# A state-space scan layer with experts: the whole causal mask inside the exponents' matrix product, in two tiles of 64 columns

## The chip, the core and the metric

One core of one Trainium2 chip runs the whole layer. Its engines are TensorE (PE, matrix products; the loading of the stationary operand is shown apart as PEld), VectorE (DVE), ScalarE (ACT), GpSimd (POOL) and SyncE (SP), which here only issues DMA transfers. The metric is the device time of one execution in microseconds; lower is better. Times of the runs shown are a median over three executions.

## The reference, cut to what matters

The layer is a state-space scan (32 heads, 64 states, head width 8, chunks of 128 steps), a pairwise gate and a mixture of eight experts. The part that the change touches is the scan inside a chunk. For each head and each chunk, `cum` is the running sum of `-dt`, and

```python
CB = jnp.einsum('bcqhn,bckhn->bchqk', C, B)
cumT = jnp.swapaxes(cum, 2, 3)
diff = cumT[..., :, None] - cumT[..., None, :]
mask = jnp.tril(jnp.ones((chunk, chunk), dtype=bool))
decay = jnp.exp(jnp.where(mask, diff, -jnp.inf))
y_intra = jnp.einsum('bchqk,bckhp->bcqhp', CB * decay, xdt)
states = jnp.einsum('bckhn,bckhp->bchpn', B * state_decay[..., None], xdt)
...
y_inter = jnp.einsum('bcqhn,bchpn->bcqhp', C * jnp.exp(cum)[..., None], prev)
```

The input is 4 sequences of 256 steps, so 8 chunks of 128 steps; the products `CB * decay` are 128x128 for each of 32 heads and 8 chunks. Ahead of it stand a projection of the input onto 4,384 rows (a product of 256 by 256 per pair of heads, in three passes of split operands) and a convolution over four steps.

## The kernel before, in words

**Prologue.** The input is normalised and turned, the first projections, z, the time steps `dt`, their running sums `cum` and the turned tokens are made. GpSimd builds constants in this time: the identity, a small table `tab`, the constant rows of the exponents' operands `cl` and `cr`, zeroed buffers, and `causal`, a 128x128 mask of ones and zeros.

**Pairs of heads.** Sixteen pairs `n` of heads follow (`over_pairs`, L249: the first written out, the next in a loop of two, the last three written out). In a pair, a step `u` from 0 to 3 is one head `j = u % 2` and one half `h = u // 2` of the chunks, that is four 128x128 blocks side by side, a tile of 128x512. For each step:

1. `exponents` (L1298) on TensorE: one product of bf16 operands, `cl[q]` (39 rows by 128) times `cr[q]` (39 rows by 512), into `bank[4 + j]`. Rows 0 to 26 carry the three bf16 parts of the running sums of both sides, rows 32 to 38 are "step rows": they add -1e30 to what lies in a block of 16 queries below the diagonal blocks of 16. So the exponent holds the mask for whole blocks of 16, and not inside the diagonal blocks.
2. `decays` (L668) on ScalarE: `dec = exp(bank)`.
3. `b_dot_c` (L1307) on TensorE, once per half: eight fp32 products of 64 rows by 128x128 into banks 2 and 3, in turn on rows 0 to 63 and 64 to 127 of the array.
4. On VectorE (L971): `g = min(dec, 1) * bank[2 + j]`, 128x512.
5. On GpSimd (L497): `g = g * causal`, in place; it raises `masked`.
6. `weigh` (L1248) on TensorE: waits for `masked`, then four fp32 products of `g` (128 rows by 128) with 16 columns each, into four bands of 32 partitions of bank 7.

Beside these steps TensorE makes the next pair's projection (`passes`: four units of six products of 128x128 by 512 columns), whose taps of the convolution are one ScalarE operation (L561) and three VectorE operations (L887) per unit. TensorE also turns B (`turn_b`), makes the new state (`new_state`), applies it (`from_state`) and turns the next weights (`turn_w`). The order on TensorE is written out by hand in `body` (L1330); between two `weigh(n, q, 0)` lies one period. In it, half 1 is `exponents` 2 and 3 and `b_dot_c(n, q, 1)` right behind them, and half 0 is `exponents` 0 and 1 of the next pair and `b_dot_c(n + 1, q, 0)`. The latter waits for the third convolution unit (`tap_done` 12n + 9).

GpSimd's order in a pair is (L492): mask 0, mask 1, `decay_c` (L490: the decayed C for the state), `prepare` (L460: three small copies for the next pair), mask 2, mask 3. In pairs 14 and 15 it also multiplies z by its gate (L503).

SyncE issues per pair: three DMAs into `cl` and one into `cr` (`load_cum`, L299), four of the result `yi` (L325, after the pair's `y` was copied), two `ecx` (L315), one `w_raw` (L290), one `taps` and two `tap_b` (L295, L297). For the first pair it waits for `const_done` 3 (L358), raised by GpSimd when `causal` is there.

**Constants before.** GpSimd writes `tab` as 32x8 and 7x128 values, and copies it out to `cr[0]` (L454, L455); ScalarE copies it to `cr[1]` (L581, L582), after `const_done` 2 and before it splits the first weights.

**After the pairs.** In the last pair (`last_pair`, L1360) TensorE mixes the scan with the output projection: `residual` (L1283) and `onto_o` (L1290). Then come the second normalisation, the router and eight experts.

Of the kernel before, what the change touches and what calls it, by code (L numbers as in the profile page):

```python
# [23 lines left out]
P = 128  # L24
# [11 lines left out]
KD = DM // P  # L36
# [16 lines left out]
BLOCK = 16  # L53
STEP0, STEPS = 32, P // BLOCK - 1


def decoder_layer(nc, x, ctx_in, W_in, conv_w, conv_b, D, z_bias, W_out, xw, xb, Wr, br, gate_bias,
# [8 lines left out]
    with ExitStack() as stack:  # L66
# [10 lines left out]
        tab = sb("tab", [STEP0 + STEPS, P])  # L77
        carry = sb("carry", [P, 2 * P])
        causal = sb("causal", [P, P])
# [39 lines left out]
        cl = [sb(f"cl{i}", [STEP0 + STEPS, 2, P], BF16) for i in range(2)]  # L119
        with ExitStack() as scan:  # L120
            cr = [scan.enter_context(nc.sbuf_tensor(f"cr{i}", [STEP0 + STEPS, 2, T, P], BF16)) for i in range(2)]
            dec = [scan.enter_context(nc.sbuf_tensor(f"dec{i}", [P, HALF], F32)) for i in range(2)]
            g = [scan.enter_context(nc.sbuf_tensor(f"g{i}", [P, HALF], F32)) for i in range(2)]
        uh = sb("uh", [P, 4, HALF], F32R)
        ul = sb("ul", [P, 4, HALF], F32R)
        xp = [sb(f"xp{i}", [P, T, 2, 2 * HD]) for i in range(2)]
# [20 lines left out]
        ewl = [sb(f"ewl{i}", [P, 3, KD, DM], F32R) for i in range(2)]  # L147
# [12 lines left out]
        gt = sb("gt", [P, T, NR, NR])  # L160
        ge = sb("ge", [P, T, NR, NR])
# [17 lines left out]
        def rows_wide():  # L179

            return tab[0:STEP0, 0:T].unsqueeze(1).unsqueeze(3).to_broadcast([STEP0, 2, T, P])

        def steps_wide():

            return tab[STEP0:STEP0 + STEPS, :].unsqueeze(1).unsqueeze(1).to_broadcast([STEPS, 2, T, P])
# [23 lines left out]
        cr1_done, cr0_done = sem("cr1_done"), sem("cr0_done")  # L209
# [15 lines left out]
        g_done, masked, y_done = sem("g_done"), sem("masked"), sem("y_done")  # L225
# [54 lines left out]
        def _(sp):  # L280
# [18 lines left out]
            def load_cum(m, q):  # L299

                at_least(sp, expo_done, 4 * (m - 2))
                for s in range(3):
                    sp.dma_start(cl[q][T * s:T * s + T, :, :],
                                 cum_dram[s, bass.ds(2 * T * (m - 1), 2 * T), :]
                                 .rearrange("(j t) k -> t j k", j=2)).then_inc(cum_in[q], 16)
# [63 lines left out]
            sp.wait_ge(cr0_done, 2)  # L369

# [41 lines left out]
        def _(pool):  # L412
# [11 lines left out]
            rows, steps_of = tab[0:STEP0, 0:T], tab[STEP0:STEP0 + STEPS, :]  # L424
            link(pool.memset(rows, 0.0))
            link(pool.memset(steps_of, NEG))
# [4 lines left out]
            link(pool.affine_select(out=steps_of, in_=steps_of, compare_op=ALU.is_ge, fill=0.0, base=0,  # L431
                                    pattern=[[1, P]], channel_multiplier=-BLOCK))
            link(pool.affine_select(out=steps_of, in_=steps_of, compare_op=ALU.is_ge, fill=0.0, base=BLOCK - 1,
                                    pattern=[[-1, P]], channel_multiplier=BLOCK))
            pool.memset(earlier[:], 1.0).then_inc(const_done, 1)
            for q in (1, 0):
                link(pool.memset(cl[q][:], 1.0))

                link(pool.affine_select(out=cl[q][STEP0:STEP0 + STEPS, :, :], in_=cl[q][STEP0:STEP0 + STEPS, :, :],
                                        compare_op=ALU.is_ge, fill=0.0, base=-BLOCK,  # L440
                                        pattern=[[0, 2], [1, P]], channel_multiplier=-BLOCK))
# [93 lines left out]
        def _(act):  # L535
# [45 lines left out]
            act.copy(cr[1][0:STEP0, :, :, :], rows_wide()).then_inc(cr1_done, 1)  # L581
            act.copy(cr[1][STEP0:STEP0 + STEPS, :, :, :], steps_wide()).then_inc(cr1_done, 1)  # L582
# [519 lines left out]
        def _(pe):  # L1102
# [426 lines left out]
```

## Time and profile before

| what | value |
|---|---|
| time, median of 3 runs (lowest to highest) | 445.43 us (443.49 to 446.92) |
| the profiled execution | 447.58 us |
| its span in the profile | 445.8 us |
| mean granted TensorE clock over the span | 0.976 of full |

The span runs from the first to the last instruction of the profiled execution; 1.8 us of its time lie around it. Busy times are the union of an engine's instructions. A product's record lasts longer than the distance between two products, since products overlap in the array, so distances between starts tell more than durations. Columns of a timeline row are: start in us, length in us, engine, line, operation, written tile <- read tiles, shapes, count merged into the row, and in brackets the idle time before it and what ended it.

### The profile page before, as it was taken

To read this page: it belongs to the slowest core of one execution; us is meant where nothing else is said; L and a number is where in the kernel's file an instruction comes from. 1 tells how busy PE (TensorE), PEld (TensorE's weight loads), DVE (VectorE), ACT (ScalarE), POOL (GpSimd) and SP (SyncE) were. 2 spreads that over 40 slices of the span, in tenths; PEclk is the share of its full clock that TensorE was granted. 3 is DMA by queue.
4 is the path that set the end of the run, shared out by engine and by line. 5 is a ranking of instruction groups with operands and counts; after the bars stand their busy time and mean duration, and the time that the engine had idled before them with its cause. 6 is when DMAs were issued, how large, how long until landed. Compare 5 with 4: busy or idle time off the path is not lost.

```text
span 445.8 us, 8885 instructions
## 1 busy us (share of the span) xinstructions
PE 414.9 (93%) x2959; PEld 318.6 (71%) x2959; DVE 351.1 (79%) x604; ACT 225.7 (51%) x408; POOL 223.3 (50%) x238
## 2 busy tenths in 40 slices
PE   2898999999999999999999977998999999999995
PEld 1686767676667676667676556766789889899885
DVE  3787689889889889889889937947886696786775
ACT  5665545455545545545577430146543653554541
POOL 3444344654544664544577540022738558648661
PEclk9999799999999999999999978999899999999999
DMA  6302101221111212112210040011110201200002
GB/s 189 77 1 53 51 8 53 57 56 55 34 28 50 56 56 56 39 23 51 54 34 32 16 137 2 1 43 50 51 48 24 73 26 45 71 0 1 0 0 96
DMA packets 33607, 20.00 MB, mean 45 GB/s; under 512 B 15816, under 2 KB 31488, under 8 KB 33584
## 3 DMA queue, kind: packets, MB, share of 16 engines
q1 hardware_dynamic: 33584, 19.71, 15.7%
q8 instruction: 13, 0.21, 0.2%
q14 instruction: 10, 0.08, 0.1%
HBM read 17.33 MB, written 1.31 MB: 42 GB/s over the span
## 4 chain that ended last, share of the span: by engine, by line
PE 43%; issue 23%; POOL 14%; DVE 12%; ACT 3%; DMA 2%; SPq 1%; POOLq 1%; DVEq 0%; ACTq 0%
PE bank L1107 30%; POOL g L497 9%; PE bank L1131 4%; DVE conv L887 4%; POOL ce L490 3%; DMA w_raw<-in_L_attn_W_in_dram 1%; PE bank L1315 1%; DVE stats L814 1%; DMA ew_raw<-in_L_ffn_Wdown_dram 1%; ACT conv L561 1%; POOL xp L462 1%; PE bank L1475 1%; PE bank L1293 1%; DVE xres L1006 1%; SPq L325 1%
## 5 line engine op out<-in xcount | busy, mean ns | idle before, releaser
L887 DVE SCALAR_TENSOR_TENSOR conv<-bank,taps,conv 128x510 f32<-128x510 f32 (+2 forms) x204 | 151.6, 746 | 28.3 <-ACT conv L561 23.5
L497 POOL TENSOR_TENSOR g<-g,causal 128x512 f32<-128x512 f32 x64 | 81.6, 1294 | 108.1 <-DVE g L971 108.1
L1131 PE MATMUL bank<-uth,parts 128*128 128x512 f32 x272 | 98.6, 413 | 1.5 <-DVE utl L870 1.0
L561 ACT ACTIVATE conv<-bank,tap_b,taps 128x512 f32<-128x512 f32 x68 | 52.9, 779 | 77.2 <-PE bank L1131 76.8
L523 POOL TENSOR_TENSOR ul<-conv,uh 128x512 fp32r<-128x512 f32 x32 | 42.8, 1353 | 46.6 <-ACT uh L770 33.7
L528 POOL TENSOR_TENSOR parts<-conv,parts 128x512 fp32r<-128x512 f32 x30 | 44.2, 1502 | 36.0 <-ACT parts L784 35.9
L1131 PEld LDWEIGHTS bank<-uth,parts 128*128 128x128 f32 x272 | 51.8, 190 | 10.7 <-issue 1.7
L1131 PE MATMUL bank<-utl,parts 128*128 128x512 f32 x136 | 56.9, 418 | 0.0
L1107 PE MATMUL bank<-ewh,parts 128*128 128x256 f32 x256 | 46.2, 279 | 1.2 <-DVE parts L1094 1.2
L1079 DVE CAST uh<-conv 128x512 fp32r<-128x512 f32 x28 | 26.4, 977 | 22.7 <-ACT conv L766 22.4
L1315 PE MATMUL bank<-conv 64*128 64x128 f32 x512 | 43.4, 289 | 0.3 <-DVE conv L887 0.3
L1315 PEld LDWEIGHTS bank<-conv 64*128 64x128 f32 x512 | 36.7, 191 | 6.8 <-DVE conv L887 5.8
L971 DVE SCALAR_TENSOR_TENSOR g<-dec,bank 128x512 f32<-128x512 f32 x64 | 40.8, 679 | 0.2 <-ACT dec L672 0.2
L1107 PEld LDWEIGHTS bank<-ewh,parts 128*128 128x128 f32 x256 | 39.6, 188 | 1.9 <-issue 1.6
L1089 DVE TENSOR_TENSOR conv<-conv 128x512 f32<-128x512 f32 x32 | 32.4, 1037 | 8.2 <-ACT conv L789 8.1
L1107 PE MATMUL bank<-ewl,parts 128*128 128x256 f32 x128 | 35.7, 279 | 0.0
L672 ACT ACTIVATE dec<-bank 128x512 f32<-128x512 f32 x64 | 34.5, 592 | 0.0
L1258 PE MATMUL bank<-g,xp 128*16 128x128 f32 x512 | 27.3, 284 | 5.7 <-POOL g L497 5.6
L1131 PEld LDWEIGHTS bank<-utl,parts 128*128 128x128 f32 x136 | 26.0, 191 | 8.8 <-issue 6.3
L766 ACT ACTIVATE conv<-bank,eb 128x512 f32<-128x512 f32 x32 | 20.1, 689 | 18.3 <-POOL eb L520 12.0
L691 ACT CAST ewh<-ew_raw 128x512 fp32r<-128x512 f32 x24 | 13.4, 617 | 30.7 <-PE bank L1107 22.4
L1062 DVE SCALAR_TENSOR_TENSOR xres<-bank,prob,xres 128x256 f32<-128x256 f32 x64 | 26.2, 472 | 2.2 <-PE bank L1107 2.2
(204 smaller groups left out, 744.0 us busy)
## 6 DMA issues: line engine op xcount, KB each, us to landing
w_raw<-in_L_attn_W_in_dram SPq DMA_DIRECT2D x17, 256.0 KB, 3.2
ecx<-ecum_dram SPq DMA_DIRECT2D x32, 128.0 KB, 2.9
ew_raw<-in_L_ffn_Wup_dram SPq DMA_DIRECT2D x7, 256.0 KB, 2.8
ew_raw<-in_L_ffn_Wgate_dram SPq DMA_DIRECT2D x7, 256.0 KB, 3.1
ew_raw<-in_L_ffn_Wdown_dram SPq DMA_DIRECT2D x7, 256.0 KB, 3.8
xres<-in_x_dram SPq DMA_DIRECT2D x2, 512.0 KB, 4.1
out_dram<-xres SPq DMA_DIRECT2D x4, 256.0 KB, 2.3
yi<-yev SPq DMA_DIRECT2D x60, 16.0 KB, 1.9
```

Source lines behind the costliest of these rows:

```text
L497: pool.tensor_tensor(g_v, g_v, causal[:].unsqueeze(1).to_broadcast([P, 4, P]), ALU.mult).then_inc(masked, 1)
L523: pool.tensor_tensor(ul[:, v, :], u32[:, v, :], f32(uh[:, v, :]), ALU.subtract).then_inc(ul_done, 1)
L528: pool.tensor_tensor(el[:, v, :], e32[:, v, :], f32(eh[:, v, :]), ALU.subtract).then_inc(el_done, 1)
L561: act.activation(conv[q][:, j, HALF * h:HALF * (h + 1)], bank[u % 2][:], ACT.Identity, bias=tap_b[q][:, j:j + 1], scale=taps[q][:, j, TAPS ...
L672: act.activation(dec[b][:], bank[4 + b][:], ACT.Exp).then_inc(exp_done, 1)
L887: dve.scalar_tensor_tensor(out=dst[:, :, d:SEQ], in0=src[:, :, 0:SEQ - d], scalar=taps[q][:, j, TAPS - 1 - d:TAPS - d], in1=dst[:, :, d:SE ...
L971: dve.scalar_tensor_tensor(out=g[b][:], in0=dec[b][:], scalar=1.0, in1=bank[2 + b][:], op0=ALU.min, op1=ALU.mult).then_inc(g_done, 1)
L1089: dve.tensor_tensor(e32[:, v, :], e32[:, v, :], u32[:, v, :], ALU.mult).then_inc(e_done, 1)
L1107: ins = pe.matmul(dst, left, right, start=(k == 0 and i == 0), stop=(k == n - 1 and i == 2))
L1131: ins = pe.matmul(bank[u % 2][:], w, x_t, start=(i == 0), stop=(i == 3 * KD - 1))
L1258: ins = pe.matmul(y_bank(n, h)[32 * i:32 * i + 2 * HD, P * h:P * (h + 1)], xp[q][:, 4 * h + i, j, :], g[j][:, i * P:(i + 1) * P], start=fi ...
L1315: ins = pe.matmul(bank[2 + j][:, i * P:(i + 1) * P], conv[q][r, 0, s], conv[q][r, 1, s], start=True, stop=True)
```

## The change

The step rows grow from 7 to 64 and `tab`, `cl` and `cr` from 39 to 96 rows. Each exponents' tile is formed by two products: keys 0 to 63 (partitions 0 to 63 of the bank) with `cr[q][0]`, and keys 64 to 127 (partitions 64 to 127) with `cr[q][1]`. Each has 96 rows, 64 stationary columns and 512 moving columns. GpSimd's multiplication by `causal` is removed, with `causal` and `masked`; `weigh` now waits for `g_done` of VectorE. `cr` is now four tiles instead of two, and GpSimd fills three of them. Each `load_cum` has five DMAs instead of four.

```diff
-BLOCK = 16
-STEP0, STEPS = 32, P // BLOCK - 1
+STEPS = NS
+ROWS = STEPS + 32
...
-        tab = sb("tab", [STEP0 + STEPS, P])
+        tab = sb("tab", [ROWS, 2, P])
-        causal = sb("causal", [P, P])
...
-        cl = [sb(f"cl{i}", [STEP0 + STEPS, 2, P], BF16) for i in range(2)]
+        cl = [sb(f"cl{i}", [ROWS, 2, P], BF16) for i in range(2)]
-            cr = [scan.enter_context(nc.sbuf_tensor(f"cr{i}", [STEP0 + STEPS, 2, T, P], BF16)) for i in range(2)]
+            cr = [[scan.enter_context(nc.sbuf_tensor(f"cr{i}_{a}", [ROWS, 2, T, P], BF16)) for a in range(2)]
+                  for i in range(2)]
...
+        ewl1 = sb("ewl1", [P, 3, KD, DM], F32R)
+        gt = sb("gt", [P, T, NR, NR])
+        ge = sb("ge", [P, T, NR, NR])
...
-                sp.dma_start(cr[q][24:27, :, :, :].rearrange("s j t k -> s (j t k)"),
-                             cum_dram[:, bass.ds(2 * T * (m - 1), 2 * T), :]
-                             .rearrange("s r k -> s (r k)")).then_inc(cum_in[q], 16)
+                for a in range(2):
+                    sp.dma_start(cr[q][a][STEPS + 3 * T:STEPS + 3 * T + 3, :, :, :].rearrange("s j t k -> s (j t k)"),
+                                 cum_dram[:, bass.ds(2 * T * (m - 1), 2 * T), :]
+                                 .rearrange("s r k -> s (r k)")).then_inc(cum_in[q], 16)
...
-            sp.wait_ge(cr0_done, 2)
...
-            rows, steps_of = tab[0:STEP0, 0:T], tab[STEP0:STEP0 + STEPS, :]
+            rows, steps_of = tab[STEPS:ROWS, 0, 0:T], tab[0:STEPS, :, :]
+            pool.wait_ge(const_done, 1)
...
-            link(pool.memset(causal[:], 1.0))
-            pool.affine_select(out=causal[:], in_=causal[:], compare_op=ALU.is_ge, fill=0.0,
-                               base=0, pattern=[[1, P]], channel_multiplier=-1).then_inc(const_done, 1)
+            for q, a in ((1, 1), (0, 0), (0, 1)):
+                link(pool.tensor_copy(cr[q][a][STEPS:ROWS, :, :, :], rows_wide()))
+                last_one = pool.tensor_copy(cr[q][a][0:STEPS, :, :, :], steps_wide(a))
+                if (q, a) != (0, 1):
+                    link(last_one)
+            last_one.then_inc(const_done, 1)
             pool.wait_ge(const_done, 3)
-            pool.tensor_copy(cr[0][0:STEP0, :, :, :], rows_wide()).then_inc(cr0_done, 1)
-            pool.tensor_copy(cr[0][STEP0:STEP0 + STEPS, :, :, :], steps_wide()).then_inc(cr0_done, 1)
-            pool.wait_ge(cr0_done, 2)
...
-                    pool.wait_ge(g_done, 4 * (n - 1) + u + 1)
-                    g_v = g[u % 2][:].rearrange("p (i k) -> p i k", k=P)
-                    pool.tensor_tensor(g_v, g_v, causal[:].unsqueeze(1).to_broadcast([P, 4, P]),
-                                       ALU.mult).then_inc(masked, 1)
...
-            act.copy(cr[1][0:STEP0, :, :, :], rows_wide()).then_inc(cr1_done, 1)
-            act.copy(cr[1][STEP0:STEP0 + STEPS, :, :, :], steps_wide()).then_inc(cr1_done, 1)
+            act.copy(cr[1][0][STEPS:ROWS, :, :, :], rows_wide()).then_inc(cr1_done, 1)
+            act.copy(cr[1][0][0:STEPS, :, :, :], steps_wide(0)).then_inc(cr1_done, 1)
...
-                pe.wait_ge(masked, a + 1)
+                pe.wait_ge(g_done, a + 1)
...
-                    pe.wait_ge(cum_in[q], 64 * (k + q))
+                    pe.wait_ge(cum_in[q], 80 * (k + q))
                 at_least(pe, exp_done, 4 * (n - 1) + u - 1)
-                pe.matmul(bank[4 + j][:], cl[q][:, j, :], cr[q][:, j, 4 * h:4 * h + 4, :].rearrange("p t k -> p (t k)"),
-                          start=True, stop=True).then_inc(expo_done, 1)
+                for a in range(2):
+                    ins = pe.matmul(bank[4 + j][NS * a:NS * (a + 1), :], cl[q][:, j, NS * a:NS * (a + 1)],
+                                    cr[q][a][:, j, 4 * h:4 * h + 4, :].rearrange("p t k -> p (t k)"), start=True, stop=True)
+                ins.then_inc(expo_done, 1)
```

The rest of the diff writes the new constants (one selection less on `tab`, one small fill more, the table twice as wide), and lets `ewl1`, `gt` and `ge`, which only the experts use, share the memory of the scan's tiles.

## Rows read from the trace of the kernel before

**Rows 1.** The page: busy time by engine; the mask's group and the exponential's.
```profile
PE 414.9 (93%) x2959; PEld 318.6 (71%) x2959; DVE 351.1 (79%) x604; ACT 225.7 (51%) x408; POOL 223.3 (50%) x238
...
L497 POOL TENSOR_TENSOR g<-g,causal 128x512 f32<-128x512 f32 x64 | 81.6, 1294 | 108.1 <-DVE g L971 108.1
```

**Rows 2.** Waits of the whole span: engine line <- releaser: us, times, longest.
```profile
PE bank L1258 <- POOL g L497: 5.6, 15, 0.4
```

**Rows 3.** Stretches from `weigh(n, q, 0)` to the next: busy us by engine, clock.
```profile
53.28:66.58 13.30, 12.91 (x116) 9.18 (x117) 11.86 (x18) 6.86 (x13) 6.83 (x9) 1.00 0.03 6
...
145.04:158.34 13.30, 12.92 (x118) 9.18 (x117) 11.81 (x18) 6.87 (x13) 6.84 (x8) 1.00 0.18 47
226.20:239.48 13.28, 12.91 (x116) 9.17 (x116) 11.76 (x18) 11.12 (x23) 10.56 (x12) 1.00 0.10 26
```

**Rows 4.** Timeline of TensorE in one pair, 144.5 to 158.5 us.
```profile
145.39 0.61 PE L1131 MATMUL bank<-uth,parts 128*128 128x512 f32 x2
146.38 0.41 PE L1258 MATMUL bank<-g,xp 128*16 128x128 f32 x8 [0.38 <-POOL g L497]
146.73 0.50 PE L1131 MATMUL bank<-utl,parts 128*128 128x512 f32 x1
147.07 0.39 PE L1131 MATMUL bank<-uth,parts 128*128 128x512 f32 x1
147.39 0.39 PE L1304 MATMUL bank<-cr,cl 39*128 39x512 bf16 x1
147.40 0.49 PE L1315 MATMUL bank<-conv 64*128 64x128 f32 x2
147.62 0.38 PE L1304 MATMUL bank<-cr,cl 39*128 39x512 bf16 x1
147.83 1.05 PE L1315 MATMUL bank<-conv 64*128 64x128 f32 x14
148.82 0.41 PE L1258 MATMUL bank<-g,xp 128*16 128x128 f32 x8
...
152.44 0.62 PE L1131 MATMUL bank<-uth,parts 128*128 128x512 f32 x2
152.99 0.41 PE L1258 MATMUL bank<-g,xp 128*16 128x128 f32 x8
...
154.44 0.60 PE L1304 MATMUL bank<-cr,cl 39*128 39x512 bf16 x2
154.91 1.16 PE L1315 MATMUL bank<-conv 64*128 64x128 f32 x16
156.01 0.41 PE L1258 MATMUL bank<-g,xp 128*16 128x128 f32 x8
```

**Rows 5.** Timelines of VectorE, GpSimd and SyncE in the same pair.
```profile
152.55 2.31 DVE L887 SCALAR_TENSOR_TENSOR conv<-bank,taps,conv 128x510 f32<-128x510 f32 x3 [0.74 <-ACT conv L561]
...
157.59 1.27 DVE L971 SCALAR_TENSOR_TENSOR g<-dec,bank 128x512 f32<-128x512 f32 x2
...
158.35 1.28 POOL L497 TENSOR_TENSOR g<-g,causal 128x512 f32<-128x512 f32 x1 [4.52 <-DVE g L971]
...
150.73 0.27 SPq L306 DMA_DIRECT2D cr<-cum_dram  x1
```

**Rows 6.** Timeline of TensorE in the prologue: L1180, four column bands at a time.
```profile
19.44 0.64 PE L1180 MATMUL bank<-uth,wa 128*32 128x256 f32 x8
19.89 0.61 PE L1180 MATMUL bank<-utl,wa 128*32 128x256 f32 x8
```

**Rows 7.** Timeline of TensorE behind the last pair: L1293, one after another.
```profile
266.95 3.62 PE L1293 MATMUL bank<-woT,yi 128*128 128x256 f32 x16
```

**Rows 8.** Timelines of GpSimd, ScalarE and SyncE in the prologue.
```profile
16.00 1.88 POOL L454 CAST cr<-tab 32x2048 bf16<-32x2048 f32 x1
...
9.00 0.59 ACT L553 CAST parts<-bank 128x512 fp32r<-128x512 f32 x1 [1.43 <-PE bank L1117]
...
36.66 0.95 SPq L303 DMA_DIRECT2D cl<-cum_dram  x3
```

**Rows 9.** Timelines of the last pair: TensorE, GpSimd.
```profile
264.17 0.50 PE L1278 MATMUL bank<-ce,state 128*16 128x128 f32 x4
264.78 0.41 PE L1258 MATMUL bank<-g,xp 128*16 128x128 f32 x8
...
262.23 2.50 POOL L497 TENSOR_TENSOR g<-g,causal 128x512 f32<-128x512 f32 x2 [5.38 <-DVE g L971]
```

**Rows 10.** The page, DMA issues: KB each, median us from issue to landing.
```profile
ecx<-ecum_dram SPq DMA_DIRECT2D x32, 128.0 KB, 2.9
```

More of the change, by code:

```diff
@@ L146, in decoder_layer @@
         ewh = [sb(f"ewh{i}", [P, 3, KD, DM], F32R) for i in range(2)]
-        ewl = [sb(f"ewl{i}", [P, 3, KD, DM], F32R) for i in range(2)]
+        ewl = [sb("ewl0", [P, 3, KD, DM], F32R), ewl1]
         eh = parts[:, 0:4, :]
@@ L159, in decoder_layer @@
         bg = sb("bg", [P, T, NR])
-        gt = sb("gt", [P, T, NR, NR])
-        ge = sb("ge", [P, T, NR, NR])
         sel = sb("sel", [P, T, NR])
@@ L179, in rows_wide, with steps_wide @@
         def rows_wide():
-            return tab[0:STEP0, 0:T].unsqueeze(1).unsqueeze(3).to_broadcast([STEP0, 2, T, P])
-        def steps_wide():
-            return tab[STEP0:STEP0 + STEPS, :].unsqueeze(1).unsqueeze(1).to_broadcast([STEPS, 2, T, P])
+            return tab[STEPS:ROWS, 0, 0:T].unsqueeze(1).unsqueeze(3).to_broadcast([ROWS - STEPS, 2, T, P])
+        def steps_wide(a):
+            return tab[0:STEPS, a, :].unsqueeze(1).unsqueeze(1).to_broadcast([STEPS, 2, T, P])
         def zgate(v):
@@ L208, in decoder_layer @@
         const_chain, const_done = sem("const_chain"), sem("const_done")
-        cr1_done, cr0_done = sem("cr1_done"), sem("cr0_done")
+        cr1_done = sem("cr1_done")
         dve_chain, act_chain = sem("dve_chain"), sem("act_chain")
@@ L224, in decoder_layer @@
         expo_done, exp_done, cb_done = sem("expo_done"), sem("exp_done"), sem("cb_done")
-        g_done, masked, y_done = sem("g_done"), sem("masked"), sem("y_done")
+        g_done, y_done = sem("g_done"), sem("y_done")
         b_turned, b_read, st_done, st_read = sem("b_turned"), sem("b_read"), sem("st_done"), sem("st_read")
@@ L302, in load_cum @@
                 for s in range(3):
-                    sp.dma_start(cl[q][T * s:T * s + T, :, :],
+                    sp.dma_start(cl[q][STEPS + T * s:STEPS + T * s + T, :, :],
                                  cum_dram[s, bass.ds(2 * T * (m - 1), 2 * T), :]
                                  .rearrange("(j t) k -> t j k", j=2)).then_inc(cum_in[q], 16)
-                sp.dma_start(cr[q][24:27, :, :, :].rearrange("s j t k -> s (j t k)"),
-                             cum_dram[:, bass.ds(2 * T * (m - 1), 2 * T), :]
-                             .rearrange("s r k -> s (r k)")).then_inc(cum_in[q], 16)
+                for a in range(2):
+                    sp.dma_start(cr[q][a][STEPS + 3 * T:STEPS + 3 * T + 3, :, :, :].rearrange("s j t k -> s (j t k)"),
+                                 cum_dram[:, bass.ds(2 * T * (m - 1), 2 * T), :]
+                                 .rearrange("s r k -> s (r k)")).then_inc(cum_in[q], 16)
             def load_ecx(m, q):
@@ L423, in _ @@
                                base=0, pattern=[[-1, P]], channel_multiplier=1).then_inc(const_done, 1)
-            rows, steps_of = tab[0:STEP0, 0:T], tab[STEP0:STEP0 + STEPS, :]
+            rows, steps_of = tab[STEPS:ROWS, 0, 0:T], tab[0:STEPS, :, :]
+            pool.wait_ge(const_done, 1)
             link(pool.memset(rows, 0.0))
-            link(pool.memset(steps_of, NEG))
+            link(pool.memset(steps_of, 0.0))
             for s in range(3):
@@ L430, in _ @@
                                         pattern=[[-1, T]], channel_multiplier=1))
[L431 to L434, printed above, removed]
+            link(pool.affine_select(out=steps_of, in_=steps_of, compare_op=ALU.not_equal, fill=NEG, base=0,
+                                    pattern=[[-(STEPS - 1), 2], [1, P]], channel_multiplier=-1))
+            link(pool.memset(tab[0:1, 1, 0:STEPS], NEG))
             pool.memset(earlier[:], 1.0).then_inc(const_done, 1)
@@ L437, in _ @@
                 link(pool.memset(cl[q][:], 1.0))
-                link(pool.affine_select(out=cl[q][STEP0:STEP0 + STEPS, :, :], in_=cl[q][STEP0:STEP0 + STEPS, :, :],
-                                        compare_op=ALU.is_ge, fill=0.0, base=-BLOCK,
-                                        pattern=[[0, 2], [1, P]], channel_multiplier=-BLOCK))
+                lower = cl[q][0:STEPS, :, :].rearrange("r j (a k) -> r j a k", a=2)
+                link(pool.affine_select(out=lower, in_=lower, compare_op=ALU.is_ge, fill=0.0, base=-1,
+                                        pattern=[[0, 2], [1, 2], [1, STEPS]], channel_multiplier=-1))
             pool.wait_ge(xn_done, 4)
```

## The prediction

> **What bounds the kernel now.** I read the page first. GpSimd's multiplication by the mask is its largest group, 64 operations of 1.294 us, 81.6 us in all, yet GpSimd is busy for only half of the span and TensorE for 93% [rows 1]. So the question is not how much is removed but how much of it anyone waits for. The waits answer that: TensorE's products of L1258 (`weigh`) stood idle for the mask 15 times, 5.6 us in all, at most 0.4 us [rows 2]. Next I cut the span into stretches from one `weigh(n, q, 0)` to the next. The first and the last of the fourteen last 13.30 and 13.28 us; TensorE is busy for 12.92 of 13.30 us, VectorE for 11.81, GpSimd for 6.84, and the granted clock is 1.00 [rows 3]. Only TensorE is near its limit, and what is missing is the one idle of 0.38 us in front of the first `weigh` of each pair [rows 4].
>
> The timeline gives that stall more exactly. In the passes two products start 0.22 to 0.23 us apart (the row at 145.39 is 0.61 long with two records of 0.39), and a `weigh` that waits for nothing starts 0.32 us after the last pass (152.44 + 0.23 = 152.67, `weigh` at 152.99). Ahead of the stalled one the last pass starts at 145.61, so it could start at 145.93 and does at 146.38: 0.45 us [rows 4]. The chain behind it is VectorE's `g` 0 and 1 at 157.59, the mask from 158.35 to 159.63, and the next `weigh` 13.30 after 146.38, at 159.68 [rows 4, 5]. The other three `weigh` of a pair wait for no mask. TensorE's own work in a period is therefore 13.30 - 0.45 = 12.85 us.
>
> **What is removed.** The stall, 0.45 us per period. `g` 0 is ready by 157.59 + 0.7 = 158.3 (two take 1.27), and TensorE reaches `weigh` at 159.23 (12.85 after 146.38), so VectorE's result is 0.9 us early and no new wait takes the place of the old one [rows 5]. VectorE itself is idle for 1.49 us of the period [rows 3], 0.74 of it in front of the third convolution unit [rows 5], so it could follow a period down to 13.30 - 0.74 = 12.56.
>
> **What is added on TensorE.** 64 products become 128, each of 64 stationary columns and 512 moving columns in bf16. Whether the two of a tile run side by side decides the sign. The nearest row is L1180, where four fp32 products with 32 columns each, in four bands of output partitions, read four different moving operands: a group of eight records starts 0.45 us after the previous one [rows 6]. The same 256 moving columns in fp32 on the whole array cost 3.62 / 8 = 0.45 us per product (16 records are eight products) [rows 7]. So four side by side took the time of one. `weigh` says the same at 128 columns. I take it that two bands of 64 columns run side by side too: an exponents' tile then costs 0.23 us as before (147.39 to 147.62) [rows 4]. The other end is one after the other, 0.46 us.
>
> What isn't free is the change of the array's shape. Before, the exponents (39 rows) and `b_dot_c` (64 rows) both use row halves and all columns. The trace shows two `b_dot_c` records starting at 147.40, beside the first exponents' product at 147.39, and only 14 left at 147.83: half 1 takes 148.82 - 147.39 = 1.43 us. In half 0, where `b_dot_c` starts behind the exponents, it alone takes 156.01 - 154.91 = 1.10 us, and the half takes 1.57 [rows 4]. With 96 rows the exponents fill all row groups, so that overlap ends: 1.57 instead of 1.43, +0.14. Then there is one more change of shape per half, between exponents and `b_dot_c`. A change costs 0.09 to 0.13 by the rows: `weigh` follows a pass by 0.32 instead of 0.23, and the pass behind it starts 0.35 after it (146.38 to 146.73) where its products alone are about 0.22, half of what L1180 takes for twice the columns [rows 4, 6]. I take 0.11 to 0.12 for each. Half 1: +0.14 + 0.11 = +0.25. Half 0: +0.12. Together +0.37 us per period. Bounds: +0.14 if changes of shape cost nothing, and about +0.8 if each also exposes the loading of weights at both ends of the exponents (0.1 a time, four times).
>
> The Trainium skill, "TensorEngine Tiling (Array Packing)", section "Tiling Modes", says that changing the tiling mode, not just the tile, drains the engine. The trace agrees with 0.09 to 0.13 us at each change of form; without the rule the sum would be 0.23 us a period better.
>
> New period: 12.85 + 0.37 = 13.22 us against 13.30, so -0.08, fourteen times: -1.1 us. Does another limit come first? The third convolution unit starts its VectorE part 0.25 us later relative to `weigh` 0 and ends at 154.86 + 0.25 = 155.11, while TensorE reaches `b_dot_c` 0 at 154.91 + 0.37 = 155.28 [rows 4, 5], so TensorE stays the limit by 0.17.
>
> **What is added on the other queues.** SyncE's `load_cum` gets one DMA more, 0.27 us of issue. The last of them ends at 150.73 + 0.27 = 151.00, now 151.27, and TensorE needs the data at 154.44 [rows 4, 5]: 3.2 us are left for it to land, so I cost it at nothing. If that cover were gone, each pair would wait for the difference. In the prologue ScalarE fills `cr[1][0]` before it splits the first weights, and stood idle for 1.43 us in front of that [rows 8]. GpSimd's start grows by a few tenths (a table twice as wide, a wait, a fill more; a selection less), within these 1.43. GpSimd then fills three tiles with six copies of 1.88 us instead of one with two [rows 8]: from about 16 us to 27.5, and the mark that SyncE needs for the first `load_cum` is read at 36.66 [rows 8]. Cost zero, with 9 us of cover. The first pair pays its added products at the start (two halves, +0.4, since its first half runs at a slower spacing) and loses its own stall (-0.3): +0.1.
>
> **The end of the pairs.** The stretch from `weigh(15, q, 0)` to the last pair's `b_dot_c` has half 1 in it: +0.25. In the last pair the masks 2 and 3 end at 262.23 + 2.50 = 264.73 and the last `weigh` starts at 264.78, behind two products that start at 264.17 [rows 9] and need about 0.27. Without the mask it starts at 264.44: -0.34, and TensorE's output projection behind it carries that on.
>
> **Sum** against the profiled execution: -1.1 + 0.1 + 0.25 - 0.34 = -1.1 us, 447.58 to 446.5. That execution lay 2.15 us above the median of the runs shown, so on the median: 445.43 - 1.1 = 444.3 us. About 1% (4.5 us) is what a measurement of this kernel can tell from no change; this is no change.
>
> **Rivals.**
> (a) The two column tiles run one after the other. The place is L1304's successor, the price 0.23 us per exponents' tile, 0.92 per period: 13.22 + 0.92 = 14.14, fourteen times +0.84 = +11.8, with the first and the fifteenth pair some +13.5, so 459 us. It decides from about 0.1 us per tile that isn't hidden: sixty-four tiles then cost 6 us, more than 1% of the time. Against it stands L1180 [rows 6, 7]; for it, that no row has bf16 with two bands of 64.
> (b) They run side by side, but each pair of them costs about 0.1 more, by an exposed load of weights or a late start of the second: four tiles, +0.4 per period, 13.62: +4.5 + 0.5, so some 449.5 us. The Trainium skill, "TensorE: Matmul & The Clock Gate", Part 3, gives 2.38 times for three column tiles at 512 columns; as an estimate from that page two tiles would cost some 0.05 more than one, +0.2 per period, 447.5 us. L1180 speaks against it.
> (c) Changes of shape are nearly free and `b_dot_c` loses only its overlap: +0.14, period 12.99, -0.31 fourteen times, -4.3, with the ends -5: 440.5 us. The 0.32 between pass and `weigh` speaks against it.
> (d) The fifth DMA makes the sums late: landing would have to take over 3.2 us where `ecx`, ten times its size, lands in 2.9 [rows 10]; a delay of 0.3 per pair gives 448.5.
>
> **Chances.** Forecast 0.55 (its own range 442 to 447.5), (a) 0.12, (b) 0.16, (c) 0.14, (d) 0.03. Faster by over 1% (below 441.0) is two thirds of (c), 0.10. Slower by over 1% (above 449.9) is (a) and half of (b), 0.20. The rest, 0.70, is within 1%. The range from 440.3 to 451 leaves out (a) and the edges.
>
> **What would show it.** Right: a period of 13.1 to 13.3 us; no wait of L1258 for anything; two exponents' records per tile starting within 0.05 us; half 1 about 1.7 us and half 0 about 1.7 us long; GpSimd's busy time down by some 82 us, up by 8 in the prologue. Wrong: exponents' records 0.2 us apart (rival a), a first `weigh` that now waits for VectorE, or a period below 13.0. Then the step at fault would be the cost of a change of shape, which I read from three distances only.

## The result, and the profile after

The changed kernel takes 443.81 us (median of 20 runs, 440.28 to 445.62) where the kernel before, run beside it, takes 445.86 us (median of 20, 443.49 to 449.06). The ratio is 0.9945 with a 95% interval of 0.9925 to 0.9966: 0.55% faster, 2.5 us, between 1.5 and 3.3. The prediction was 444.3 us on a median of 445.43, so -1.1 us forecast and -2.5 measured. By the bound of 1% it is no change, as forecast; with 20 runs on each side it can be told from none.

The page first: busy time by engine, and the groups that answer to [rows 1].

```profile
PE 415.7 (94%) x3023; PEld 314.9 (71%) x3023; DVE 348.5 (79%) x604; ACT 225.6 (51%) x408; POOL 150.6 (34%) x176
...
L491 POOL TENSOR_TENSOR ce<-conv,ecx 128x512 f32<-128x512 f32 x16 | 20.9, 1306 | 157.7 <-DVE conv L884 157.7
L1255 PE MATMUL bank<-g,xp 128*16 128x128 f32 x512 | 27.7, 284 | 0.0
```

GpSimd fell from 223.3 to 150.6 us (81.6 of mask gone, 8.9 come in, 7.5 of it four more copies of constants). That is worth next to nothing by itself. TensorE has 64 products more and nearly the same busy time (414.9 us before, 415.7 now). The last row is the effect: `weigh` (now L1255) has no idle time before it, where it stood 5.6 us in fifteen waits [rows 2].

The chain that ended last, by engine, has no GpSimd in it any more, where GpSimd had 14% of it before:

```profile
PE 84%; DVE 9%; DMA 3%; ACT 2%; issue 1%; SPq 1%; DVEq 0%; ACTq 0%
```

The stretches from one `weigh(n, q, 0)` to the next, as in [rows 3]: length, busy us of PE, PEld, DVE, ACT and POOL, clock, DMA.

```profile
52.94:66.11 13.17, 13.17 (x121) 9.05 (x120) 11.75 (x17) 6.83 (x14) 1.46 (x3) 1.00 0.04 8
131.98:145.15 13.17, 13.17 (x121) 9.05 (x120) 11.76 (x17) 6.86 (x14) 1.75 (x5) 1.00 0.18 48
224.20:237.37 13.17, 13.17 (x122) 9.05 (x121) 11.76 (x17) 11.11 (x22) 8.34 (x11) 1.00 0.12 29
```

A period lasts 13.17 us instead of 13.30, and TensorE is busy in all of it. The starts of the first and the fifteenth `weigh(n, q, 0)`, 52.94 and 237.37, give 13.174 over fourteen periods. So the stall of 0.45 us is gone and 0.32 us of work on TensorE has taken its place. TensorE's timeline in one pair shows where (as [rows 4], 132 to 142 us).

```profile
131.98 0.41 PE L1255 MATMUL bank<-g,xp 128*16 128x128 f32 x8
132.32 0.50 PE L1128 MATMUL bank<-utl,parts 128*128 128x512 f32 x1
132.66 0.40 PE L1128 MATMUL bank<-uth,parts 128*128 128x512 f32 x1
132.98 0.62 PE L1302 MATMUL bank<-cr,cl 96*64 96x512 bf16 x4
133.54 1.16 PE L1314 MATMUL bank<-conv 64*128 64x128 f32 x16
134.63 0.41 PE L1255 MATMUL bank<-g,xp 128*16 128x128 f32 x8
...
140.28 0.62 PE L1302 MATMUL bank<-cr,cl 96*64 96x512 bf16 x4
140.83 1.16 PE L1314 MATMUL bank<-conv 64*128 64x128 f32 x16
141.92 0.41 PE L1255 MATMUL bank<-g,xp 128*16 128x128 f32 x8
```

Four exponents' products and the change of shape behind them take 0.56 us (132.98 to 133.54) where two products took 0.44 in half 1 (147.39 to 147.83) and 0.47 in half 0 [rows 4]: the two bands run side by side. The two records of a tile start within 0.02 us of each other. All sixteen records of `b_dot_c` now stand behind the exponents, none beside them. Half 1 lasts 134.63 - 132.98 = 1.65 us (1.43 before) and half 0 141.92 - 140.28 = 1.64 (1.57 before): +0.22 and +0.07, +0.29 in all.

### The profile page after: what moved, and what is told of

It reads as the page before. It is cut to its first block, busy times and chain, and to the rows that moved or that the text cites. A ratio compares the mean times of both kernels' runs of the same rounds, so it can differ in the third digit from the quotient of the medians.

```text
span 443.9 us, 8932 instructions
## 1 busy us (share of the span) xinstructions
PE 415.7 (94%) x3023; PEld 314.9 (71%) x3023; DVE 348.5 (79%) x604; ACT 225.6 (51%) x408; POOL 150.6 (34%) x176
## 4 chain that ended last, share of the span: by engine, by line
PE 84%; DVE 9%; DMA 3%; ACT 2%; issue 1%; SPq 1%; DVEq 0%; ACTq 0%
PE bank L1104 30%; PE bank L1128 22%; PE bank L1314 8%; PE bank L1255 5%; PE bank L1302 4%; PE bank L1264 3%; PE bank L1322 2%; PE bank L1114 2%; PE bank L1275 2%; DVE conv L884 2%; DMA w_raw<-in_L_attn_W_in_dram 1%; PE bank L1290 1%; DMA ew_raw<-in_L_ffn_Wdown_dram 1%; DVE stats L811 1%; PE bank L1474 1%
## 5 line engine op out<-in xcount | busy, mean ns | idle before, releaser
L491 POOL TENSOR_TENSOR ce<-conv,ecx 128x512 f32<-128x512 f32 x16 | 20.9, 1306 | 157.7 <-DVE conv L884 157.7
L1104 PE MATMUL bank<-ewh,parts 128*128 128x256 f32 x256 | 47.2, 282 | 1.2 <-DVE parts L1091 1.2
L1314 PEld LDWEIGHTS bank<-conv 64*128 64x128 f32 x512 | 31.7, 191 | 13.7 <-issue 7.2
L1314 PE MATMUL bank<-conv 64*128 64x128 f32 x512 | 37.9, 288 | 0.3 <-DVE conv L884 0.3
L688 ACT CAST ewh<-ew_raw 128x512 fp32r<-128x512 f32 x24 | 13.4, 618 | 33.1 <-PE bank L1104 24.4
L1255 PE MATMUL bank<-g,xp 128*16 128x128 f32 x512 | 27.7, 284 | 0.0
```

The source lines that it names most:

```text
L1104: ins = pe.matmul(dst, left, right, start=(k == 0 and i == 0), stop=(k == n - 1 and i == 2))
L1255: ins = pe.matmul(y_bank(n, h)[32 * i:32 * i + 2 * HD, P * h:P * (h + 1)], xp[q][:, 4 * h + i, j, :], g[j][:, i * P:(i + 1) * P], start=fi ...
L1314: ins = pe.matmul(bank[2 + j][:, i * P:(i + 1) * P], conv[q][r, 0, s], conv[q][r, 1, s], start=True, stop=True)
```

## The experiments

Each kernel is measured beside runs of the kernel before on the same chip; where its own number of runs is small (4 to 6 for most), the period in its trace, fourteen times repeated, tells more than its median.

### 1. What the mask alone cost

The kernel before without GpSimd's multiplication; the mask inside the diagonal blocks is left out.

```diff
-                    pool.wait_ge(g_done, 4 * (n - 1) + u + 1)
-                    g_v = g[u % 2][:].rearrange("p (i k) -> p i k", k=P)
-                    pool.tensor_tensor(g_v, g_v, causal[:].unsqueeze(1).to_broadcast([P, 4, P]),
-                                       ALU.mult).then_inc(masked, 1)
...
-                pe.wait_ge(masked, a + 1)
+                pe.wait_ge(g_done, a + 1)
```

> The kernel before, without GpSimd's multiplication (the mask inside the diagonal blocks of 16 is left out of the computation), the exponents as they were. Theory (TensorE's order bounds the pairs, the mask cost one stall of 0.45 us a pair): the period falls from 13.30 to 12.85 us, no wait takes the stall's place, fourteen times -0.45 and the ends some -0.6, so about 439 us, ratio 0.985. Rival (VectorE or a DMA takes over): a new idle before the first weigh or before b_dot_c, period 13.0 to 13.2, 442 to 444 us.

437.06 us, ratio 0.9784 (0.9729 to 0.9838). The stretch of all fourteen periods, with the same columns as above:

```profile
51.92:231.65 179.73, 179.73 (x1625) 128.62 (x1624) 164.62 (x238) 100.01 (x191) 30.32 (x60) 1.00 0.17 44
```

179.73 / 14 = 12.84 us, against 12.85 expected. TensorE is busy throughout and nothing takes the stall's place. This is the most that a free mask could bring in the periods: 0.46 us each, 6.5 us. The change brought 0.13 each. The median fell by more than that, 8.5 us; in this trace the last pair is 3.0 us shorter as well (22.65 us against 25.64), and the part on the last pair, behind the experiments, says why that stretch varies.

### 2. What the new exponents alone cost

The changed kernel with the mask's multiplication, its constant and its semaphore put back.

> The changed kernel with GpSimd's multiplication by the mask put back. Theory (the path from weigh 0 over half 1, the third unit's passes, ScalarE, VectorE and the mask back to weigh 0 is one closed chain of 13.30 us, and the new half 1 is 0.22 longer): period 13.52 us, fourteen times +0.22, about 449 us. Rival (the stall of 0.45 us is slack that swallows the added 0.3 us of TensorE): period stays 13.30, 446 us.

450.01 us (ten runs), ratio 1.0082 (1.0048 to 1.0116).

```profile
51.15:240.97 189.82, 185.16 (x1681) 126.73 (x1681) 164.68 (x239) 100.64 (x191) 99.98 (x116) 1.00 0.16 43
```

The stall in front of `weigh` 0 is back; in this kernel `weigh` is L1263 and the mask L502:

```profile
132.50 0.41 PE L1263 MATMUL bank<-g,xp 128*16 128x128 f32 x8 [0.34 <-POOL g L502]
```

189.82 / 14 = 13.56 us, +0.26 against before (+0.22 expected). The stall did not swallow the added work: TensorE is idle again for 0.33 us a period (185.16 of 189.82). So the stall was no slack. It closed a chain in which half 1 itself stands (`weigh` 0, half 1, the third unit's passes, its convolution, `g` 0, the mask, `weigh` 0), and what is added to half 1 comes out again behind the mask. Half 0 stands beside that chain: VectorE still works on the convolution when its `b_dot_c` is done. Its 0.07 us are missing from the 0.26, which fits. Exponents +0.26 with the mask, +0.33 without (13.17 against 12.84), mask +0.46 with the old exponents and +0.39 with the new.

### 3. Do the two bands run side by side?

Both products of a tile sent to the same partitions, hence to the same columns of the array (the exponents of keys 64 to 127 go astray).

```diff
-                    ins = pe.matmul(bank[4 + j][NS * a:NS * (a + 1), :], cl[q][:, j, NS * a:NS * (a + 1)],
+                    ins = pe.matmul(bank[4 + j][0:NS, :], cl[q][:, j, NS * a:NS * (a + 1)],
```

> The changed kernel with both exponents' products of a tile sent to partitions 0 to 63 of the bank, so that they use the same column band and must run one after the other (the exponents of keys 64 to 127 are left out of the right place). Theory (two bands run side by side and save the whole second product): each of four tiles costs 0.22 us more, period 13.17 + 0.9 = 14.07 us, about 457 us. Rival (the bands only overlap in part): under 0.15 us per tile, period below 13.8, below 453 us.

456.34 us, ratio 1.0214 (1.0154 to 1.0275). TensorE's timeline of one half:

```profile
130.11 1.05 PE L1302 MATMUL bank<-cr,cl 96*64 96x512 bf16 x4
131.09 1.16 PE L1314 MATMUL bank<-conv 64*128 64x128 f32 x16
132.19 0.41 PE L1255 MATMUL bank<-g,xp 128*16 128x128 f32 x8
```

The four products take 0.98 us until `b_dot_c` starts, against 0.56 side by side: 0.42 more for two tiles, 0.21 a tile, which is a whole product. The period is (247.52 - 51.34) / 14 = 14.01 us, 14.07 expected. So the bands save a whole product; rival (a) is refuted, and it would have cost 0.84 us a period (14.01 against 13.17) where the prediction said 0.92. Experiment 4 has the other comparison, two bands against one product.

### 4. Rows or bands: what costs the 0.3 us?

One product of 96 rows and 128 columns in place of the two (the mask of keys 64 to 127 is wrong).

```diff
-                for a in range(2):
-                    ins = pe.matmul(bank[4 + j][NS * a:NS * (a + 1), :], cl[q][:, j, NS * a:NS * (a + 1)],
-                                    cr[q][a][:, j, 4 * h:4 * h + 4, :].rearrange("p t k -> p (t k)"), start=True, stop=True)
+                ins = pe.matmul(bank[4 + j][:], cl[q][:, j, :],
+                                cr[q][0][:, j, 4 * h:4 * h + 4, :].rearrange("p t k -> p (t k)"), start=True, stop=True)
```

> The changed kernel with one product per tile, 96 rows and all 128 columns, on the first of the two cr tiles (the mask of keys 64 to 127 is left out). The array keeps the shape of the passes, so the change of shape between passes and exponents falls away and the one before b_dot_c stays. Theory (what the change costs TensorE is the lost overlap with b_dot_c plus one more change of shape of about 0.1 us per half): period 13.17 - 0.2 = 12.97 us, about 441 us. Rival (the loss is all in the overlap, shape changes between passes and exponents are free): period 13.1 to 13.2, 443 to 444 us.

439.05 us, ratio 0.9848 (0.9789 to 0.9907).

```profile
128.99 0.41 PE L1255 MATMUL bank<-g,xp 128*16 128x128 f32 x8
129.91 0.61 PE L1301 MATMUL bank<-cr,cl 96*128 96x512 bf16 x2
130.44 1.16 PE L1313 MATMUL bank<-conv 64*128 64x128 f32 x16
131.54 0.41 PE L1255 MATMUL bank<-g,xp 128*16 128x128 f32 x8
...
137.08 0.61 PE L1301 MATMUL bank<-cr,cl 96*128 96x512 bf16 x2
137.64 1.16 PE L1313 MATMUL bank<-conv 64*128 64x128 f32 x16
138.73 0.41 PE L1255 MATMUL bank<-g,xp 128*16 128x128 f32 x8
```

From `weigh` to the exponents it is 0.92 us instead of 1.00: the change of shape between passes and exponents is gone, 0.08. But from the exponents to the next `weigh` it is 1.63 in half 1 and 1.65 in half 0, nearly the changed kernel's 1.65 and 1.64 and not the 1.43 and 1.57 of before. Counted from the exponents on, the 96 rows alone lengthen the halves: the sixteen records of `b_dot_c` stand behind the exponents here too. The halves leave out what lies in front of the exponents, though, and there the bands cost something. The period is (232.87 - 51.10) / 14 = 12.98 us, 12.97 expected, so the three kernels without a mask form a ladder:

| exponents | period us | step |
|---|---|---|
| 39 rows, 128 columns (experiment 1) | 12.84 | |
| 96 rows, 128 columns (this one) | 12.98 | +0.14, the rows |
| 96 rows, two bands of 64 columns (the change) | 13.17 | +0.19, the bands |

The rows cost 0.14 us, the overlap of `b_dot_c` with the exponents. They add no change of shape: the one in front of the exponents moves behind them. The bands bring the second change of shape in each half, and that is the larger part of the 0.33.

### 5. The same stall, removed by order alone

If the mask costs one stall in front of `weigh` 0, two passes in between cover it, with the mask where it was. The same move saves a change of shape, and can be made for `weigh` 2 and `from_state` as well. Both moves were put into both kernels.

```diff
-                passes(m, r, 1, range(4))
+                passes(m, r, 1, range(6))
                 weigh(n, q, 0)
-                passes(m, r, 1, range(4, 6))
...
-                passes(m, r, 3, range(4))
+                passes(m, r, 3, range(6))
                 weigh(n, q, 2)
                 from_state(n, 0)
                 from_state(n, 1)
-                passes(m, r, 3, range(4, 6))
```

> The kernel before, mask and all, with the first weigh of a pair moved two passes later, in front of exponents 2 and 3. Theory (the mask cost one stall of 0.45 us, and each change of shape of the array about 0.1): the stall is covered by the two passes (0.46 us) and the array goes from weigh to exponents without the passes between, which saves 0.2 more: period 12.84 - 0.2 = 12.65 us, fourteen times -0.65, about 436.5 us, better than both kernels. Rival (the closed chain over VectorE and GpSimd, 13.30 us, does not get shorter by it): period 13.1 to 13.3, 443 to 446 us.

> The same with weigh 2 and from_state also moved two passes later, in front of the next pair's exponents. Theory: TensorE's own order falls by another 0.2 us to 12.45, but the chain over VectorE and the mask (13.30 - 0.67 = 12.63 us) then sets the period: 12.6 us, about 436 us, and a stall for the mask of 0.1 to 0.2 us is back. Rival (only TensorE's order counts): 12.45 us, 433.5 us.

> The changed kernel with the first weigh moved two passes later. Theory (one change of shape less): period 13.17 - 0.2 = 12.97 us, about 441 us. Rival (changes of shape cost only together with waits, so nothing is gained where weigh doesn't wait): period 13.17, 443.8 us.

> The changed kernel with weigh 0, weigh 2 and from_state two passes later. Theory: two changes of shape less, period 13.17 - 0.4 = 12.77 us, about 438.3 us, still behind the kernel before in the new order. Rival (VectorE's chain, at least 12.6, interferes): 12.9 or more, 440 us.

| kernel | median us (runs) | ratio, interval | period us, expected |
|---|---|---|---|
| before, weigh 0 later | 440.41 (4) | 0.9834, 0.9741 to 0.9927 | 12.78, 12.65 |
| before, both later | 436.70 (4) | 0.9767, 0.9701 to 0.9832 | 12.66, 12.6 |
| after, weigh 0 later | 440.95 (4) | 0.9864, 0.9798 to 0.9930 | 12.93, 12.97 |
| after, both later | 439.01 (4) | 0.9835, 0.9764 to 0.9906 | 12.86, 12.77 |

The stretch of fourteen periods of the kernel before with both moves, and behind it that of the changed kernel with both:

```profile
52.69:229.92 177.23, 176.23 (x1625) 130.77 (x1625) 164.48 (x239) 101.96 (x192) 99.39 (x116) 1.00 0.18 45
```

The changed kernel:

```profile
51.04:231.01 179.97, 179.04 (x1681) 128.89 (x1680) 164.41 (x239) 101.99 (x192) 30.71 (x61) 1.00 0.18 45
```

With the two moves the old kernel, GpSimd's mask and all, has a period of 12.66 us: below the changed kernel's 13.17, and below 12.84, what the mask's removal alone gave. This is not the cover alone, since the moves also save changes of shape: the changed kernel, which had no stall, gains 0.31 by them (13.17 to 12.86).

The first move was 0.13 us a period short of its forecast in the kernel before. The two passes cover the mask but for a rest:

```profile
127.80 0.39 PE L1131 MATMUL bank<-uth,parts 128*128 128x512 f32 x1
128.25 0.41 PE L1258 MATMUL bank<-g,xp 128*16 128x128 f32 x8
```

`weigh` 0 follows the last pass by 0.45 us, where it is 0.32 in the changed kernel in the same order (128.50 to 128.82), and starts 0.07 us after its mask ends (126.89 + 1.29 = 128.18). `weigh` 2 is 0.11 us late in the same way. Half of these 0.24 us come back in half 0, where `b_dot_c` starts 0.36 us after the exponents instead of 0.47. The list of waits shows none of this in the fourteen periods, because the records of the passes last longer than the gap.

On the changed kernel the first move is worth 0.24 us (13.17 to 12.93): that is what going in and out of the passes' shape costs once less. It is more than the 0.1 of one change, because the first pass behind `weigh` also holds up the next one, by 0.34 us instead of 0.23 (132.32 to 132.66 in the timeline of the changed kernel). The second move is worth only 0.07, since now `b_dot_c` 0 waits for the third convolution unit, which VectorE ends at 133.87 + 2.31 = 136.18:

```profile
135.54 0.62 PE L1302 MATMUL bank<-cr,cl 96*64 96x512 bf16 x4
136.23 1.16 PE L1314 MATMUL bank<-conv 64*128 64x128 f32 x16
```

That is 0.69 us instead of 0.55. In the kernel before with both moves it is 0.68 instead of 0.47, and the first `weigh` follows its pass by 0.34. So its period of 12.66 hit the forecast of 12.6, but the wait in it is for VectorE in front of `b_dot_c` and not the one for the mask that was expected.

### 6. The last pair, and the versions that beat both

In the last pair ScalarE stands for the first expert's weights, whose three DMAs wait on SyncE behind the result of pair 15. ScalarE's timeline in the kernel before (L691), the wait in brackets:

```profile
259.90 0.62 ACT L691 CAST ewh<-ew_raw 128x512 fp32r<-128x512 f32 x1 [8.35 <-DMA ew_raw<-in_L_ffn_Wdown_dram]
```

And in the changed kernel (L688):

```profile
258.37 0.62 ACT L688 CAST ewh<-ew_raw 128x512 fp32r<-128x512 f32 x1 [8.75 <-DMA ew_raw<-in_L_ffn_Wdown_dram]
```

The exponentials and everything behind them wait with it. I moved these loads to the end of SyncE's turn for pair 15, in four settings (the definition of `load_expert` moves ahead of the loop with them).

```diff
                 if n + 2 <= PAIRS:
                     load_taps(n + 2, q)
+                if n == PAIRS - 1:
+                    load_expert(0, 0)
...
-            load_expert(0, 0)
```

> The kernel before in the new order of both moves, with the three loads of the first expert's weights issued at the end of pair 15's turn on SyncE instead of behind the last result's DMAs. Theory (in the last pair ScalarE stands 7 to 9 us for these weights, and the exponentials behind it, g, the masks and the last weigh with it): that wait goes, VectorE's gating is next, the last pair gets 3 to 5 us shorter, 432 to 433.5 us. Rival (the stretch is bound by the result's DMAs and VectorE anyway): under 1 us, 436 us.

> The changed kernel in the same order and with the same early loads. Theory: period 12.86 us as without the early loads, so 2.8 us slower than the other in the fourteen pairs, and up to 1.5 us faster in the last pair, where no mask stands between g and the last weigh once the weights are there: 433.5 to 435.5 us. Rival (the last pair hides the masks behind VectorE's gating): the whole 2.8 us stay, 435 to 436.5 us.

> The kernel before in its own order, with only the first expert's weights loaded early. Theory (the wait of ScalarE for these weights ends the last pair, with two masks behind it): period 13.30 us as ever, last pair from weigh(15, q, 0) to the residual some 21.8 us instead of 25.6, about 442.5 us. Rival (something else ends the last pair): over 24 us, 445 us or more.

> The changed kernel in its own order, with only the early loads. Theory (the wait for the weights hid what the masks cost the last pair): period 13.17 us, last pair some 19.0 to 19.3 us, so 1.8 us from the periods and 2.5 us from the last pair ahead of the other kernel of this call, 438 to 439 us. Rival (the change is worth no more than its 2 us in any setting): 440.5 us or more.

| kernel, with the early loads | median us (runs) | ratio, interval | last pair us |
|---|---|---|---|
| before, own order | 443.23 (12) | 0.9948, 0.9927 to 0.9969 | 21.77 |
| after, own order | 439.25 (6) | 0.9858, 0.9828 to 0.9888 | 19.70 |
| before, both later | 435.64 (5) | 0.9753, 0.9726 to 0.9780 | 21.76 |
| after, both later | 433.81 (5) | 0.9705, 0.9679 to 0.9732 | 19.03 |

The last pair is counted from `weigh(15, q, 0)` to the last four of the residual's products (in the new order it therefore starts two passes later); without the early loads it lasts 265.12 - 239.48 = 25.64 us before and 263.72 - 237.37 = 26.35 after. In all four of these last pairs the granted clock is 1.00. With the weights in time the masks stand in the open. The kernel before with the early loads, TensorE in the last pair:

```profile
257.99 0.41 PE L1258 MATMUL bank<-g,xp 128*16 128x128 f32 x8 [1.01 <-POOL g L497]
258.23 0.40 PE L1278 MATMUL bank<-ce,state 128*16 128x128 f32 x4
259.22 0.41 PE L1258 MATMUL bank<-g,xp 128*16 128x128 f32 x8 [0.60 <-POOL g L497]
259.56 1.99 PE L1287 MATMUL bank<-xres,ident 128*128 128x256 f32 x8
```

TensorE at the same place in the changed kernel with them:

```profile
254.28 0.50 PE L1255 MATMUL bank<-g,xp 128*16 128x128 f32 x9
...
255.06 1.99 PE L1284 MATMUL bank<-xres,ident 128*128 128x256 f32 x8
```

Two waits of 1.01 and 0.60 us are there in the first and absent in the second. In their own order the change is now worth 4.0 us (443.23 to 439.25): fourteen times 0.13 and 21.77 - 19.70 = 2.1 in the last pair, together 3.9. In the new order the two are level: the changed kernel is 2.95 us behind in the fourteen periods (180.17 us against 177.22) and 2.73 ahead in the last pair, and the spans of the two traces are 434.8 and 435.1 us. The medians differ by 1.8 us, with intervals that meet at the edge (0.9679 to 0.9732 and 0.9726 to 0.9780), and that difference goes with the clock: four of the changed kernel's five executions had a mean granted clock of 0.991 to 0.996 and took 432.4 to 434.45 us, the fifth had 0.980 and took 436.59; the other kernel's five had 0.980 to 0.984 and took 434.18 to 437.01. That the change has a part in the higher clock isn't shown. So 433.81 us is the lowest median found, 3% below before, and that it beats 435.64 by the change is not shown.

Not all that the last pair gains is kept. In the own order it is 3.87 us shorter (25.64 to 21.77), but the stretch from the residual to the end grows from 180.68 to 182.24 us, and the median against the kernel before falls by 2.1. In the new order the kernel before gains 3.06 us in the last pair (24.82 to 21.76) and that stretch grows from 180.66 to 183.90, at a granted clock of 0.96 instead of 0.98; its forecast of 432 to 433.5 us was missed, and the rival, under 1 us, came nearer. What lengthens the stretch behind was not traced.

## Why the prediction was right

**The bound.** "Only TensorE is near its limit": experiment 1 shows it, 12.84 us with TensorE busy in all of it, where 12.85 was read from the distances between starts. The idle time that the waits gave, 0.38, would have said 12.92; the distances were the better reading, since a product's record reaches past the start of the next.

**The bands.** That two bands of 64 columns run side by side was taken from L1180, four bands of fp32. Experiment 3 shows that in turn they cost 0.21 us more a tile, and experiment 4 that side by side two tiles take 0.56 and 0.55 us until `b_dot_c` starts, where one product per tile takes 0.53 and 0.56.

**The change of shape, mis-sized.** The step was "+0.37 us per period", from +0.25 for half 1 and +0.12 for half 0. The rows say +0.22 and +0.07. In the period it is 0.33 (12.84 to 13.17), of which 0.04 lies outside the two halves and is not placed. The lost overlap (+0.14) was right, by experiment 4 (12.84 to 12.98). The two changes of shape were taken at 0.23 together, 0.11 to 0.12 each by a choice within 0.09 to 0.13; over the period they are 0.19 (12.98 to 13.17), and between exponents and `b_dot_c` the rows show 0.07 to 0.09 for one (0.56 - 0.47, 0.55 - 0.47). The Trainium skill, "TensorEngine Tiling (Array Packing)", section "Tiling Modes", names the drain without a price; the trace agrees with the rule at 0.08 us. The period came out at 13.17 instead of 13.22, which is 0.7 us of the 1.4 that the forecast was off. The upper bound of +0.8, which added an exposed load of weights at each end of the exponents, was not needed: no such load shows.

**The other queues.** The six copies of GpSimd were hidden, and the fifth DMA was not waited for: no wait of TensorE for a DMA stands in the pairs. The stretch from `weigh(15, q, 0)` to the last pair's `b_dot_c` cost 0.18 us more (239.48 to 248.06, 237.37 to 246.13) where +0.25 was forecast. The first pair, from the first exponents to the first `weigh`, was 0.38 us longer (48.02 to 53.28 before, 47.30 to 52.94 after) where +0.1 was forecast, but the two stretches had different clocks, 0.87 granted before and 0.78 after: the two halves at its start took 0.70 us more (forecast +0.4), and the stall's loss gave back 0.32 (forecast 0.3). How much of the 0.70 is the clock isn't separated.

**The last pair, wrong.** "Without the mask it starts at 264.44: -0.34". The last `weigh` did lose its wait for the mask, but the pair didn't get shorter, 26.35 us against 25.64. One part is the weights' DMA, which took 5.45 us from its issue in the changed kernel's profile and 4.21 in the other; ScalarE's first operation on the weights came 0.58 us later after `weigh(15, q, 0)`. The other part is the clock. From that operation to the residual it is 5.22 us before and 5.35 after, +0.13 and not -0.34. In the changed kernel TensorE waited 4.58 us for ScalarE and then ran with a granted clock of 0.50, the 1.2 GHz level, up to the residual; before, it waited 2.63 us, and the same stretch had 0.67:

```profile
259.33 0.40 PE L1275 MATMUL bank<-ce,state 128*16 128x128 f32 x2 [4.58 <-ACT state L684]
...
260.30 2.07 PE L1290 MATMUL bank<-woT,yi 128*128 128x256 f32 x4
262.30 0.82 PE L1255 MATMUL bank<-g,xp 128*16 128x128 f32 x9
...
263.72 2.51 PE L1284 MATMUL bank<-xres,ident 128*128 128x256 f32 x8
```

The four products of the output projection in front of the last two `weigh` take 2.07 us here and 1.13 with the early loads (253.22 in that trace). The traces without early loads line up by the clock of this stretch. Without a mask it takes 3.34 us at 1.00 (experiment 1), 4.29 at 0.75 (experiment 4), 4.84 to 4.92 at 0.65 (experiments 5 and 3) and 5.35 at 0.50 to 0.51; with the masks it takes 5.20 to 5.42 at 0.67 to 0.72. So at nearly the same clock, 0.65 to 0.67, the masks cost 0.3 to 0.4 us, as forecast, and in these two traces the slower clock of the changed kernel took that back. I had seen the weights' wait and priced only the last `weigh`. Experiment 6 shows the size of that term with the wait gone and the clock at 1.00: 2.1 us in the own order and 2.7 in the new one.

**What stays open, and what was luck.** In the two profiled executions the time to the first exponents differs by -0.72 us, the first pair by +0.38, the fourteen periods by -1.77, the last pair by +0.71 and the rest behind it by -0.50, -1.9 in all. Only the periods come out the same in the second trace of each kernel (with the early loads, 13.30 and 13.17), and -1.77 is what the change is shown to bring. The forecast had -1.1 for them and -1.1 in all. That the whole came so near to it is in part luck: the first and the last pair came out longer than forecast, and the stretches ahead of and behind the pairs, to which it gave nothing, shorter. The medians say -2.5, between -1.5 and -3.3; the periods alone lie in that interval, and the 0.7 beyond them is not explained. Single executions differ by more: the first `weigh` stands anywhere between 50.94 and 53.28 us in the traces here. The clock's mean doesn't explain it: over the twenty executions of the changed kernel it is 0.984, and 0.984 too over those of the kernel before that ran beside the experiments.

**The rivals.** (a) is refuted by experiment 3. (b), 0.1 us more for each pair of bands, is refuted by experiment 4: at most 0.03 for two tiles. (c), that changes of shape are free, is refuted by experiment 4 and by experiment 5, where one less gained 0.24 us with no stall to cover, though the truth lay on its side of the forecast. Of (d) the trace shows nothing: no wait of TensorE for these DMAs stands in the pairs.

## What to carry to other kernels

An engine that waits for another in one place of a periodic order has a closed chain behind that wait; before the work is removed, see whether two independent instructions in front of the wait cover it. Here the new order brought the old kernel to 12.66 us a period, where this way of removing the mask brought 13.17; about 0.3 of that are changes of shape saved, and in the new order the change costs 0.2. A product that fills more rows of the array can cost nothing itself and still cost its neighbours their overlap: look for records that start beside each other before the number of rows is raised (0.14 us a period here). Splitting the columns adds a change of shape where the neighbour in front uses all of them (0.19 us a period here). And a stretch that waits for a DMA hides what its other steps cost, and a lower clock behind that wait (0.50 granted here) hides more of it, so a change should be priced again when that DMA is made early.

## What the runs showed of the hardware that was not expected

Records of `b_dot_c`, whose products take 64 rows, start while an exponents' product of 39 rows runs (147.40 beside 147.39 [rows 4]), and don't once the exponents have 96 rows. That the early ones are the product on the other half of the rows fits, but the trace doesn't name the half. In half 1 that overlap and the missing change of shape are worth 0.22 us, as much as one whole product of 512 columns (0.21); in half 0, where nothing overlapped, the change of shape alone is worth 0.07. Two 64-column bf16 products of 512 columns in different bands cost as much as one of 128 columns, to within 0.03 us: two tiles until `b_dot_c` starts take 0.56 and 0.55 us (132.98 and 140.28 in the changed kernel) against 0.53 and 0.56 (129.91 and 137.08 in experiment 4).
